# A decoder block kernel on one core: the order of work in the six local attention layers

## What is computed

```python
for i in range(DEPTH):                       # 6
    x = attn_layer(shift_tokens(x), Wqkv[i], q_scale[i], k_scale[i], Wo[i]) + x
    x = ffn_layer(shift_tokens(x), ln_g[i], ln_b[i], W1[i], b1[i], W2[i], b2[i]) + x
...
def attn_layer(x, Wqkv, qs, ksc, Wo):
    q, k, v = ...                            # 16 heads of 64
    q, k = l2norm(q) * qs, l2norm(k) * ksc   # then rotated with scaled tables
    sim = q k^T * 8, masked to windows of 32 that also look at the window before
    return (softmax(sim) v) @ Wo
def ffn_layer(x, ...):
    xn = layernorm(x) ; a, gate = split(xn @ W1 + b1)
    return a * gelu(gate) @ W2 + b2
```

## Time and profile before

| | us |
|---|---|
| median of 3 runs | 3883.37 |
| lowest, highest | 3873.95, 3886.67 |
| the profiled execution | 3868.69 |
| its span, first to last instruction | 3866.8 |

### The profile page before, as it was taken

The page is one execution under the profiler, slowest core; times in us unless marked ns, Lnnn a source line. Parts: engine busy times, 40 slices in busy tenths (PEclk is TensorE's granted clock), DMA queues, the critical chain, the costliest instruction groups (busy, mean ns, idle before and its releaser), DMA issues. The chain is left out here.

```text
span 3866.8 us, 92494 instructions
## 1 busy us (share of the span) xinstructions
PE 3266.6 (84%) x38586; PEld 2285.0 (59%) x38586; DVE 2639.8 (68%) x4547; ACT 1970.1 (51%) x3554; POOL 1275.3 (33%) x844
## 2 busy tenths in 40 slices
PE   7585898999999998766639767999999997999996
PEld 4455655777777776731114344666666665667774
DVE  5424475666666666369986787888888874777773
ACT  1331344555555554359971234665665653446553
POOL 1102204555555553410022145666556651000000
PEclk9686788999999999787878888999999998989998
DMA  1023301000000000720000102121121111000000
GB/s 41 5 72 99 113 1 40 2 10 1 10 1 1 2 1 7 246 76 1 1 5 1 47 26 87 49 56 37 49 57 35 32 27 43 11 20 20 11 2 12
DMA packets 88712, 131.17 MB, mean 34 GB/s; under 512 B 18450, under 2 KB 60106, under 8 KB 87532
## 3 DMA queue, kind: packets, MB, share of 16 engines
q1 hardware_dynamic: 85292, 119.03, 10.9%
q0 software_dynamic: 3008, 6.23, 0.4%
HBM read 86.63 MB, written 10.94 MB: 25 GB/s over the span
## 5 line engine op out<-in xcount | busy, mean ns | idle before, releaser
L2847 POOL TENSOR_TENSOR wide_probs<-wide_probs,wide_factor 128x1024 f32<-128x1024 f32 x128 | 239.6, 1893 | 310.9 <-ACT wide_factor L2808 310.9
L2804 ACT ACTIVATE wide_probs<-wide_ps_s,wide_nm 128x1024 f32<-128x1024 f32 (+1 forms) x256 | 237.1, 926 | 172.0 <-DVE wide_nm L2889 152.3
L175 POOL TENSOR_TENSOR model_Y<-model_Y,model_X 128x512 f32<-128x512 f32 x12 | 15.2, 1269 | 930.9 <-POOLq L66 930.9
L2884 DVE TENSOR_REDUCE wide_nm<-wide_ps_s 128x1 f32<-128x1024 f32 x128 | 155.9, 1219 | 195.3 <-PE wide_ps_s L2690 195.3
L2355 ACT ACTIVATE narrow_probsT<-narrow_ps 128x512 f32<-128x512 f32 (+1 forms) x448 | 220.1, 582 | 134.0 <-PE narrow_ps L2259 131.4
L3994 POOL TENSOR_TENSOR local_turn<-local_turn 128x1024 f32<-128x1024 f32 x96 | 226.7, 2368 | 158.3 <-DVE local_turn L4052 157.8
L2409 DVE TENSOR_REDUCE narrow_part<-narrow_ps 128x1 f32<-128x512 f32 x384 | 242.2, 684 | 45.7 <-PE narrow_ps L2242 43.1
L3208 DVE TENSOR_TENSOR bonds_strain<-peri_in_moved 128x1664 f32<-128x1664 f32 (+3 forms) x128 | 257.0, 2083 | 1.1 <-PEq L66 1.1
L3259 PE MATMUL bonds_ps<-bonds_act_of,bonds_out 128*32 128x448 f32 (+3 forms) x1024 | 153.3, 696 | 117.5 <-ACT bonds_act_of L3232 84.3
L2702 PE MATMUL wide_ps<-model_ident,wide_probs 128*128 128x128 f32 (+1 forms) x1664 | 238.9, 274 | 10.8 <-DVE wide_probsT L2894 9.1
L2242 PE MATMUL narrow_ps<-second_KQ 32*128 32x512 f32 x768 | 242.1, 653 | 1.2 <-ACT second_KQ L2326 1.0
(11 more groups left out here) (650 smaller groups left out, 8383.3 us busy)
## 6 DMA issues: line engine op xcount, KB each, us to landing
moe_w<-in_L_ffn_w SPq DMA_DIRECT2D x62, 512.0 KB, 4.8
local_V<-local_V SPq DMA_DIRECT2D x96, 128.0 KB
e_wqkv<-in_L_ffn_qkv SPq DMA_DIRECT2D x6, 1536.0 KB, 8.1
local_V<-local_V SPq DMA_DIRECT2D x144, 64.0 KB
context_rows<-in_ctx SPq DMA_DIRECT2D x8, 768.0 KB
e_keys<-in_ctx_T SPq DMA_DIRECT2D x6, 800.5 KB, 4.5
e_source<-in_ctx_T SPq DMA_DIRECT2D x4, 800.5 KB, 5.0
second_source<-in_ctx_T SPq DMA_DIRECT2D x4, 800.5 KB, 6.2
```

The costliest lines, as they stand in the source:

```text
L2804: act.activation(probs[:, n % 2, h, lo:hi], ps_s[h][:, 0:hi - lo], ACT.Exp, bias=nm[:, n % 2, h, 2 * half:2 * half + 1], scale=1.0, accum_ ...
L2847: pool.tensor_tensor(v, v, factor[:, n // 4 % 2, j:j + 1].broadcast_to([P, CUT]), ALU.mult).then_inc(lowered[i].sem, 1)
```

## The change

Only the order of steps in `rounds()` changes; no instruction is added or taken out.
- "inv" of tile r - 2 and the value products "o" of tile r - 2 move from behind the scores "s" to behind "sum", in the middle of the round.
- "qt" of tile r - 1 moves from in front of "sum" to behind "o".
- The turn "ot" and the output projection "wo" now belong to tile r - 2, the one whose "o" stands in the same round, where they belonged to tile r - 3 before. "ot" stands behind "v" (before: in front of it), "wo" stays where it was.

```diff
             if r % 2:
                 shift, last = (r - 5) // 2, (r - 7) // 2
-                yield from [("gm", shift), ("k", r), ("pt", r - 2), ("gd", last), ("qt", r - 1), ("sum", r), ("ot", r - 3), ("xs", last),
-                            ("root", r), ("v", r), ("gv", shift), ("inv", r - 2), ("s", r - 1), ("rest", r), ("wo", r - 3), ("o", r - 2), ("gx", shift)]
+                yield from [("gm", shift), ("k", r), ("pt", r - 2), ("gd", last), ("sum", r), ("inv", r - 2), ("o", r - 2), ("qt", r - 1), ("xs", last),
+                            ("root", r), ("v", r), ("ot", r - 2), ("gv", shift), ("s", r - 1), ("rest", r), ("wo", r - 2), ("gx", shift)]
             else:
                 g = (r - 6) // 2
-                yield from [("k", r), ("pt", r - 2), ("ga", g), ("gb", g), ("qt", r - 1), ("sum", r), ("ot", r - 3), ("root", r), ("v", r),
-                            ("inv", r - 2), ("s", r - 1), ("rest", r), ("wo", r - 3), ("o", r - 2), ("sh", (r - 4) // 2)]
+                yield from [("k", r), ("pt", r - 2), ("ga", g), ("gb", g), ("sum", r), ("inv", r - 2), ("o", r - 2), ("qt", r - 1), ("root", r),
+                            ("v", r), ("ot", r - 2), ("s", r - 1), ("rest", r), ("wo", r - 2), ("sh", (r - 4) // 2)]
```

## The result

The changed kernel takes 4065.93 us (median of 4 runs, 4060.81 to 4069.94) beside 3878.66 us for the kernel before (3873.59 to 3886.67): ratio 1.0506, 95% interval 1.0470 to 1.0541, 187 us slower. The forecast was 4055 us.

The account below looks back on a forecast made before the run. PE paced rounds of 17.45 us, hiding a four-engine loop of 16.9 and 16.8 us that the change lengthens to a mean 20.7. Profiled 3868.7 + 144 (loop) + 28 (clock) = 4041, as median 4055 us; range 4005 to 4100.

Parts of the forecast that it names:

- rival C: Round loop: only the direct wait for turn and scores counts, 19.1 us a round, +78, 3961 us; chance 0.07.
- D: PE at the turn: O is evicted in time, no wait arises, idle time closes; 3861 us; chance 0.04.
- E: Whole round: PE is busiest and no instruction is added, so it stays 17.45 us; 3883 us; chance 0.03.
- A: PE's clock: stays at 1.00, so only the loop's +144 counts; 4027 us; chance 0.26.
- B: Clock falls every round at full price, half the gate's wait stays in 21 even rounds: +144 + 71 + 13, 4111; chance 0.10.
- The loop's links: Chain through all four engines from one mask addition to the next: 20.6 us in even rounds, 20.8 in odd.
- L4050 waiting for L3931: DVE's q waits for ACT's square of q, expected about 1.9 us a round in the profile after.
- hidden with 1.8 us to spare: DVE's sh or gx after the mask addition: 4.9 and 4.5 us of work under the chain's 6.7 us.
- The terms put into it: Added to the loop: O's eviction 1.27 us, turn 0.9, scores 1.52, and gv 0.6 in odd rounds.
- The clock, +28 us: PE behind its wait for O: clock falls each even and every other odd round, 31.5 x 0.9 us.
- The slot planner: PSUM slots: new neighbours delay PE by at most 1 us, nothing on the loop, at most +0.3 a round.
- The tail: Stretch behind the last scores: loses one product's wait, taken as 0, between -4 and +2.

Follow-up runs that it names:

- a_v_twice: The changed kernel with the value projection made twice over, 1.9 us more PE work a round in front of its wait for O; 4044.2 us, ratio 1.0458.
- b_v_twice: The kernel before with the value projection made twice over, 1.9 us more PE work a round; 3919.2 us, ratio 1.0154.
- a_q_first: The changed kernel with ACT squaring q of tile r before it takes the exponential of tile r - 2; 4050.1 us, ratio 1.0469.
- a_ot_twice: The changed kernel with the turn of O made twice over, output unchanged; 4110.9 us, ratio 1.0640.
- a_ot_behind_s: The changed kernel with the turn of O behind the score products instead of in front of them; 4110.1 us, ratio 1.0615.
- its twin: The changed kernel with the turn of O behind the scores, plus a planner hold of 3 for o that alters only PSUM slots; 4007.2 us, ratio 1.0365.
- a_q_first_short_gx: The changed kernel with q squared before the exponential and the second DVE step of gx left out; ratio 1.0457.
- c_order: The kernel before with its own order (q squared before the exponential, turn, scores and value products moved) and new planner holds; ratio 1.0008.

## Why the prediction was right

**The bound moved from PE to a loop.** Right. a_v_twice against b_v_twice shows it by the times, the link table by the trace. Direct wait alone (rival C, 3961), faster (D) and no change (E) are excluded by the result. A (no clock, 4027) is excluded by the granted clock of 0.96; of B (4111) neither part came: half clock reached 16 of 40 rounds, not every one, and DVE's wait in front of the gate products fell from 11.1 to 3.1 us in the 700 us. The upper end of the range, called two thirds of the way to B, would have been 4092 and not 4100 by that working.

**The loop's links, 20.6 and 20.8 us.** The first three are right within 0.25 us in both kinds of round. L4050 waiting for L3931 was expected to show 1.9 us a round; the trace shows 24 us in 13 rounds, because gx and sh stretched under POOL until they just filled the cover. The length was right and the slack was not: "hidden with 1.8 us to spare" is the step that failed, harmless in the changed kernel, and it is why a_q_first gained nothing in the rounds with gx.

**The terms put into it.** O's eviction 1.27, the turn 0.9, gv 0.6, scores 1.52: right in an undisturbed round (3.89 us for 3.69 in even, 4.45 for 4.29 in odd rounds). The turn's price was measured by itself in a_ot_twice, 0.84 to 0.87 us in undisturbed rounds.

**The clock, +28 us.** Right in kind, too large in size. It fell where it was expected to, behind the idle time in front of the turn, for 52 of the 155 us that lie between O and L4061 in 40 rounds. It had been laid out for each even and every other odd round; it came in 14 of 20 even and 2 of 20 odd ones. Its price can only be bounded: what is left of the last link over an undisturbed one, once the stops are taken off, is 0.66 us an even and 0.09 an odd round, some 17 us over 46 rounds; a_v_twice, with hardly any half clock, gained 9 us without the stops. So 9 to 17 us stand where 28 were put.

**What was missing.** No term stood for PE's stops, which have no releaser in the list of waits. They stood in the list of waits of before, mostly in the value products where they cost little. In the last link they are 0.75 us an even and 0.38 an odd round, some 26 us over 46 rounds. The undisturbed last link is 0.2 us longer than laid out, 8 us, and the first three links add 4.

**Some luck in the sum.** 144 + 28 made 172; measured are 187 by the medians and 199 by the spread of the mask additions in the profiled execution. By the trace the terms are 144 + 17 + 26 + 8 + 4 = 199. So the loop, the large term, was right, but the clock's term, put too high, made good a part of what was left out.

**The slot planner.** "Nothing on the loop" held for the changed kernel, as the first three links show. That it can hold or not by a single number is what a_ot_behind_s and its twin show: 103 us apart with one and the same order.

**The tail.** Taken at 0, between -4 and +2. From the last mask addition to the last residual of the layers (L4110) it is 40.9 us before and 42.1 after: +1.2.

## What to carry to other kernels

Before moving an eviction and its consumer close together, follow one tile's chain around all engines until it comes back to where it began, and add the new links to that loop, not to the busiest engine: here 3.7 to 4.3 us went into a loop that had 0.6 us to spare, while the wait they removed was 0.9. When a planner gives out buffers by order, look at who had each buffer last after every reordering, since a wait that the order avoids can come back through the buffer. To tell whether an engine or a loop sets the pace, double one of the engine's steps where it idles and see whether the time grows. And check what is late next before pricing a removed link: of 1.8 us freed in a_q_first_short_gx 1.1 were given back.

## What was not expected of the hardware

PE's 128 small products with their weight loads (1.48 us) can be cut by stops of 0.4 to 2.5 us with no semaphore behind them: 36 stops in 96 such bursts before the change, 3 of them of 1.4 us or more; 33 after it, 23 of them of 1.4 us or more. Each ended 1.08 to 1.63 us behind the landing of an instruction load. Small edits move them: with the turn doubled (a_ot_twice) the scores lost 2.9 us to stops instead of 24.8, and an order without other waits (c_order) has 35.6 us of idle time without a releaser on this line in the stretch instead of 17.1. DVE's two steps of gx take 0.48 and 0.35 us alone and 1.99 and 1.83 beside POOL's work. And more work for PE in its idle time did not slow the kernel down but made it, as far as the noise lets one say, 14 to 22 us faster, with the clock at its upper level and fewer stops.
